# Gate and up projections of two token tiles by Strassen's scheme: seven products of quarters in place of eight

## The reference

```python
def fp4_quant_dequant(x):
    xb = x.reshape(shape[:-1] + (shape[-1] // BLOCK, BLOCK))     # BLOCK = 16
    scale = jnp.maximum(jnp.max(jnp.abs(xb), axis=-1, keepdims=True) / 6.0, 1e-12)
    q = _GRID[jnp.searchsorted(_MID, jnp.abs(xb / scale))] * jnp.sign(xb / scale) * scale
gate = fp4_linear(x, w_gate)          # 8192 tokens x 512, weights 1408 x 512
y = fp4_linear(x, w_up)
h = jax.nn.silu(gate) * y
return fp4_linear(h, w_down)          # 1408 -> 512
```

## Time and profile before

| | before |
|---|---|
| runs | 2209.19, 2212.1, 2213.11 us; median 2212.1 us |
| the profiled execution | 2211.99 us, its span 2209.8 us, mean granted clock 0.998 |
| busy: PE, DVE, POOL, ACT | 97%, 75%, 55%, 30% of the span |
| chain that ended last | PE 89%, DVE 4%, issue 3% |
| DMA | 251.82 MB, mean 114 GB/s |

### The profile page before, as it was taken

One profiled execution on the slowest core, in us unless ns is written; L12 is line 12 of the kernel. 1 busy time (PEld: TensorE's weight loads), 2 busy tenths in 40 slices (PEclk: granted clock), 3 DMA queues, 4 the chain that ended last, 5 costly groups with the idle time before them and its releaser, 6 DMA issues.

```text
span 2209.8 us, 46872 instructions
## 1 busy us (share of the span) xinstructions
PE 2152.9 (97%) x16712; PEld 1045.1 (47%) x16712; DVE 1663.1 (75%) x3108; ACT 657.1 (30%) x1009; POOL 1219.6 (55%) x877
## 2 busy tenths in 40 slices
PE   4999999999999989999999999999999999999999
PEld 1445454544545444444444444444444444444444
DVE  7777878778687665778778777787787877878774
ACT  3233333333343322222222222222222232222221
POOL 3266767676675544555555555555555555555553
PEclk9999999999999999999999999999999999999999
DMA  9656666585756444333333433333334333343333
GB/s 270 175 124 177 156 148 180 125 198 127 181 151 167 131 137 129 78 90 80 87 83 79 94 75 85 89 81 87 83 77 91 78 87 84 77 92 76 87 74 68
DMA packets 449418, 251.82 MB, mean 114 GB/s; under 512 B 367282, under 2 KB 373938, under 8 KB 449300
## 3 DMA queue, kind: packets, MB, share of 16 engines
q1 hardware_dynamic: 448404, 246.99, 46.0%
q10 hardware_dynamic: 576, 2.10, 0.2%
q0 software_dynamic: 320, 0.97, 0.2%
HBM read 99.01 MB, written 59.77 MB: 72 GB/s over the span
## 4 chain that ended last, share of the span: by engine, by line
PE 89%; DVE 4%; issue 3%; DMA 1%; SPq 1%; POOL 1%; ACT 0%; DVEq 0%; POOLq 0%; ACTq 0%
PE acc L977 19%; PE prj L1345 7%; PE ops L1345 7%; PE prj L977 6%; PE acc L1326 5%; PE acc L1330 5%; PE acc L1327 5%; PE prj L1347 3%; PE ops L1347 3%; PE acc L1328 2%; PE sps L1328 2%; PE sps L1331 2%; PE acc L1331 2%; PE sps L1329 2%; PE acc L1329 2%
## 5 line engine op out<-in xcount | busy, mean ns | idle before, releaser
L977 PE MATMUL acc<-late 128*128 128x512 f16 x2304 | 518.8, 382 | 15.0 <-DMA late<-xh 10.4
L977 PEld LDWEIGHTS acc<-late 128*128 128x128 f16 x2304 | 220.9, 98 | 281.8 <-issue 21.2
L208 POOL TENSOR_TENSOR qk<-qk,xh 128x1408 f32<-128x1408 f32 x64 | 165.7, 2590 | 230.0 <-DVE qk L245 230.0
L1220 DVE SCALAR_TENSOR_TENSOR qk<-acc,row_gains,xh 128x512 f32<-128x512 f32 x64 | 48.0, 751 | 260.4 <-ACT xh L1285 260.4
L203 POOL TENSOR_TENSOR qk<-qk,xh 128x1024 f32<-128x1024 f32 (+1 forms) x128 | 177.5, 1387 | 111.1 <-DVE xh L224 111.1
L213 POOL TENSOR_TENSOR v<-qk,v 128x1408 f16<-128x1408 f32 x64 | 183.1, 2860 | 100.3 <-ACT v L255 100.3
L1345 PE MATMUL prj<-late,qk 128*128 128x512 f16 x704 | 214.6, 379 | 0.7 <-DMA qk<-v 0.7
L1345 PE MATMUL ops<-late,qk 128*128 128x512 f16 x704 | 214.6, 379 | 0.0
L255 ACT ACTIVATE v<-qk 128x1408 f16<-128x1408 f32 x64 | 88.1, 1377 | 367.4 <-POOL qk L208 367.4
L1326 PE MATMUL acc<-late,turned 128*128 128x512 f16 x512 | 194.0, 379 | 0.4 <-DVE qk L1220 0.4
L1330 PE MATMUL acc<-late,turned 128*128 128x512 f16 x512 | 194.0, 379 | 0.0
(11 more groups left out here) (158 smaller groups left out, 4440.8 us busy)
## 6 DMA issues: line engine op xcount, KB each, us to landing
normed<-late SPq DMA_DIRECT2D x64, 256.0 KB, 2.7
res<-in_L_attn_x SPq DMA_DIRECT2D x64, 256.0 KB, 3.1
attended<-res SPq DMA_DIRECT2D x64, 256.0 KB, 2.6
raw<-normed SPq DMA_DIRECT2D x64, 256.0 KB, 2.7
v<-attended SPq DMA_DIRECT2D x64, 256.0 KB, 2.7
out<-v SPq DMA_DIRECT2D x64, 256.0 KB, 2.0
late<-in_L_attn_x SPq DMA_DIRECT2D x62, 256.0 KB, 3.9
ready<-turned SPq DMA_DIRECT2D x36, 256.0 KB, 2.3
```

Source lines behind the costliest of these rows:

```text
L208: pool.tensor_tensor(blocks(v), blocks(v), spread(s[3]), ALU.mult).then_inc(q["valued"], 1)
L977: last = pe.matmul(out, lhsT, rhs, start=(at == 0), stop=(at == n - 1))
```

## The change

Two tiles A1, A2 (rows) and their 512 channels are seen as a matrix of four quarters: a tile is a row of quarters, its channels 0 to 255 and 256 to 511 the columns. Gate and up of the weights are likewise four quarters, by channel half and by gate or up. The seven products of the Winograd form of Strassen's scheme give all four results (gate and up of both tiles), with four sums of rows, four sums of weights and seven sums of products a chunk.

- Weights: `sum_units` on POOL forms four sums of 128 x 256 for each group of gate and up units; four splits (4, 4, 6 and 4 blocks of 128) replace three, so `ready` and the places of the weights (`weight_places`) hold 14 blocks for gate and up where there were 8. The step strings of attention are new on all engines.
- Rows: both tiles of a pair are loaded, scaled with a joint row gain (`joint_gain`), and split in seven quarters (`low_rows`, `LEFT = 7`), after `sum_rows` on DVE.
- Products: `products` makes seven products of six matmuls a chunk. ACT copies the first three to SBUF (`copy_product`, tile `mc`). POOL adds `second_sum`, `fourth_sum` and `second_up`; DVE adds `third_sum`, `first_gate`, `first_up` and `second_gate`, each from a PSUM bank and an SBUF tile. `hidden` reads up and Silu from SBUF for both tiles. `freed` is what a bank's next product waits for.
- The hidden tile is quantised whole, 1408 columns at a time, in place of 1024 and 384.
- `periods` becomes `pairs`, which runs a step string for a pair of tiles: letter, number (tile of the pair, chunk or product), prime for the pair before, plus for the next one. On POOL `a`, `b`, `e` are the three sums, `s`, `v`, `l` rows, `S`, `V`, `L` hidden tiles. On DVE `m`, `j`, `q`, `w` are the rows' maxima, gain, rounding and sums; `u`, `g`, `c`, `d` the four sums from PSUM; `x`, `y` the hidden products; `B`, `Q`, `K` the hidden maxima, gain and rounding; `f` closes a tile.

The first gate and up products no longer stand in attention's list of TensorE, but in feed-forward's. The core of the diff:

```diff
-def periods(engine, step):
-
-    for t in range(4):
-        step(t - t % 2, t % 2)
-    with engine.Fori(2, NT // 2 - 2) as pair:
-        for k in range(2):
-            step(pair * 2, k)
-    for t in range(NT - 4, NT + DRAIN):
-        step(t - t % 2, t % 2)
+def pairs(engine, steps, do, begun):
+
+
+    def follow_pair(pair, q):
+        for step in steps.split():
+            shift = step.count("+") - step.count("'")
+            if isinstance(pair, int) and (not 0 <= pair + q + shift < NT // 2 or
+                                          pair + q + shift == 0 and step[0] in begun):
+                continue
+            do[step[0]](pair + (q + shift), (q + shift) % 2, int(step[1:].strip("+'")))
+
+    for pair in (0, 2):
+        for q in range(2):
+            follow_pair(pair, q)
...
-    dve.tensor_reduce(g[:, 0:1], s[1], AX.X, ALU.max).then_inc(q["row"], 1)
...
+        def sum_units(b, n):
+            g, half = n // 2, C // 2
+            (b11, b21), (b12, b22) = ((raw[:, m, 0:half], raw[:, m, half:]) for m in range(2))
+            if n % 2 == 0:
+                pool.wait_ge(f["valued"], at(b, PER, 3 * g + 1))
+                pool.wait_ge(f["low"], at(b, SPLITS, 4 * g))
+                pool.tensor_tensor(b11, b12, b11, ALU.subtract).then_inc(f_sum, 1)
+                pool.wait_ge(f_sum, at(b, SPLITS, 4 * g))
+                pool.tensor_tensor(b12, b22, b12, ALU.subtract).then_inc(f_sum, 1)
+            else:
+                pool.wait_ge(f["low"], at(b, SPLITS, 4 * g + 1))
+                pool.tensor_tensor(b12, b22, b11, ALU.subtract).then_inc(f_sum, 1)
+                pool.wait_ge(f_sum, at(b, SPLITS, 4 * g + 2))
+                pool.tensor_tensor(b21, b21, b12, ALU.subtract).then_inc(f_sum, 1)
+
+        def low_split(b, n):
+            pool.wait_ge(f["high"], at(b, SPLITS, n))
+            to = split_of(wh, n)
+            pool.tensor_tensor(to[:, 1], sources(n), to[:, 0], ALU.subtract).then_inc(f["low"], 1)
...
+        def turn_rows(p, q, n):
+            since(sp, xq["low"], p * 3 + (2 + n))
+            hold(sp, held)
+            since(sp, made, p * 21 - 21)
+            if second(p) and n == 0:
+                await_all(sp, ended.projected + ended.everything)
+            hold(sp, held)
+            lo, hi = (0, 3) if n == 0 else (3, LEFT)
+            sp.dma_start_transpose(xt[q][:, lo:hi].rearrange("p m a c t -> p (m a c) t"),
+                                   xh[:, lo:hi].rearrange("p m a c -> p (m a c)")).then_inc(xt_in[q], 16)
+
...
+        def low_rows(p, q, n):
+            if n == 0:
+                since(pool, xq["high"], p * 3 + 2)
+                pool.tensor_tensor(xh[:, 0:2, 1, :], halves(xr[:, 0, :]), xh[:, 0:2, 0, :],
+                                   ALU.subtract).then_inc(xq["low"], 1)
+                pool.tensor_tensor(xh[:, 2, 1, :], xr[:, 1, C // 2:], xh[:, 2, 0, :],
+                                   ALU.subtract).then_inc(xq["low"], 1)
+            else:
+                since(pool, xq["high"], p * 3 + 3)
+                pool.tensor_tensor(xh[:, 3:LEFT, 1, :], halves(xr.rearrange("p k c -> p (k c)")), xh[:, 3:LEFT, 0, :],
+                                   ALU.subtract).then_inc(xq["low"], 1)
+
+        def second_sum(p, q, c):
+            since(pool, copied, p * 9 + (3 * c + 2))
+            n = CHUNKS[c][1]
+            pool.tensor_tensor(mc[:, c % 2, 1, 0:n], mc[:, c % 2, 1, 0:n], mc[:, c % 2, 0, 0:n],
+                               ALU.add).then_inc(u2_done, 1)
+
+        def fourth_sum(p, q, c):
+            since(pool, copied, p * 9 + (3 * c + 3))
+            since(pool, u2_done, chunk(p, c))
+            since(pool, hq["low"], tile(p, 0) - 4)
+            if second(p) and c == 0:
+                await_all(pool, ended.projected)
+            s, n = cols(c)
+            pool.tensor_tensor(hv[q][:, 0, s], mc[:, c % 2, 1, 0:n], mc[:, c % 2, 2, 0:n], ALU.add).then_inc(u4_done, 1)
+
+        def second_up(p, q, c):
+            since(pool, u3_done, chunk(p, c))
+            since(pool, copied, p * 9 + (3 * c + 3))
+            since(pool, u4_done, chunk(p, c))
+            s, n = cols(c)
+            pool.tensor_tensor(mc[:, c % 2, 2, 0:n], hv[q][:, 1, s], mc[:, c % 2, 2, 0:n], ALU.add).then_inc(up1_done, 1)
+
+        def scale_hidden(p, q, k):
+            scale(pool, hq, hv[q][:, k, :], [hs[:, k, n, :] for n in range(4)], tile(p, k) - 1)
+
+        def value_hidden(p, q, k):
+            since(pool, hq["gained"], tile(p, k))
+            value(pool, hq, hv[q][:, k, :], [hs[:, k, n, :] for n in range(4)], tile(p, k) - 1)
+
+        def low_hidden(p, q, k):
+            low(pool, hq, hv[q][:, k, :], hh, tile(p, k) - 1)
...
+        def joint_gain(p, q, n):
+            g = xg[:, q, :]
+            since(dve, xq["scales"], p * 2 + 2)
+            dve.tensor_reduce(g[:, 0:1], xs[:, :, 1, :], AX.XY, ALU.max).then_inc(xq["row"], 1)
+            row_gain(dve, xq, g, p)
+            dve.tensor_scalar(xs[:, :, 3, :], xs[:, :, 1, :], g[:, 2:3], -SUM_TOP,
+                              ALU.mult, ALU.mult).then_inc(xq["gained"], 1)
+            dve.tensor_tensor(g[:, 3:4], g[:, 1:2], wsc[:, 4:5], ALU.mult).then_inc(xq["gains"], 1)
+
+        def round_rows(p, q, k):
+            rounded(dve, xq, xr[:, k, :], xm, tile(p, k) - 1)
...
+        def sum_rows(p, q, n):
+            h = C // 2
+            a11, a12, a21, a22 = xr[:, 0, 0:h], xr[:, 0, h:], xr[:, 1, 0:h], xr[:, 1, h:]
+            since(dve, xq["low"], p * 3 + 2)
+            dve.tensor_tensor(a22, a21, a22, ALU.add).then_inc(summed, 1)
+            dve.tensor_tensor(a21, a11, a21, ALU.subtract).then_inc(summed, 1)
+            since(dve, summed, p * 4 + 2)
+            dve.tensor_tensor(a11, a22, a11, ALU.subtract).then_inc(summed, 1)
+            since(dve, summed, p * 4 + 3)
+            dve.tensor_tensor(a12, a12, a11, ALU.subtract).then_inc(summed, 1)
+
+        def third_sum(p, q, c):
+            if c == 0 and (first(p) or second(p)):
+                await_all(dve, ended.attended if first(p) else ended.projected)
+            s, n = cols(c)
+            since(dve, made, product(p, c, 3))
+            since(dve, u2_done, chunk(p, c))
+            since(dve, hq["low"], tile(p, 1) - 4)
+            dve.tensor_tensor(hv[q][:, 1, s], bank(q, c, 3)[:, 0:n], mc[:, c % 2, 1, 0:n], ALU.add).then_inc(u3_done, 1)
+
+        def first_gate(p, q, c):
+            n = CHUNKS[c][1]
+            since(dve, made, product(p, c, 4))
+            since(dve, copied, p * 9 + (3 * c + 1))
+            since(dve, h_done[0], chunk(p, before(c)))
+            dve.tensor_tensor(sg[:, c % 2, 0, 0:n], bank(q, c, 4)[:, 0:n], mc[:, c % 2, 0, 0:n], ALU.add).then_inc(gate0_done, 1)
+
+        def first_up(p, q, c):
+            s, n = cols(c)
+            since(dve, made, product(p, c, 5))
+            since(dve, u4_done, chunk(p, c))
+            dve.tensor_tensor(hv[q][:, 0, s], bank(q, c, 5)[:, 0:n], hv[q][:, 0, s], ALU.add).then_inc(up0_done, 1)
+
+        def second_gate(p, q, c):
+            s, n = cols(c)
+            since(dve, made, product(p, c, 6))
+            since(dve, u3_done, chunk(p, c))
+            since(dve, h_done[1], chunk(p, before(c)))
+            dve.tensor_tensor(sg[:, c % 2, 1, 0:n], bank(q, c, 6)[:, 0:n], hv[q][:, 1, s], ALU.add).then_inc(gate1_done, 1)
+
+        def hidden(p, q, c, k):
+            s, n = cols(c)
+            since(dve, xq["gains"], p + 1)
+            if k == 0:
+                since(dve, up0_done, chunk(p, c))
+            else:
+                since(dve, up1_done, chunk(p, c))
+                since(dve, gate1_done, chunk(p, c))
+            since(dve, silu_done[k], chunk(p, c))
+            up = mc[:, c % 2, 2, 0:n] if k else hv[q][:, 0, s]
+            dve.scalar_tensor_tensor(hv[q][:, k, s], up, xg[:, q, 3:4], sg[:, c % 2, k, 0:n],
...
+                                     ALU.mult, ALU.mult).then_inc(h_done[k], 1)
...
+        def hidden_maxima(p, q, k):
+            since(dve, h_done[k], chunk(p, 2))
+            since(dve, hq["valued"], tile(p, k) - 2)
+            block_scales(dve, hq, hv[q][:, k, :], [hs[:, k, n, :] for n in range(4)], 1e-12,
+                         tile(p, k) - 1)
+
+        def hidden_gain(p, q, k):
+            g, s = hg[:, k, :], [hs[:, k, n, :] for n in range(4)]
+            since(dve, hq["scales"], tile(p, k))
+            dve.tensor_reduce(g[:, 0:1], s[1], AX.X, ALU.max).then_inc(hq["row"], 1)
+            row_gain(dve, hq, g, tile(p, k) - 1)
+            dve.tensor_scalar(s[3], s[1], g[:, 2:3], -SCALE_TOP, ALU.mult, ALU.mult).then_inc(hq["gained"], 1)
+            since(dve, final, tile(p, k) - 4)
+            dve.tensor_tensor(hk[:, 2 * q + k:2 * q + k + 1], g[:, 1:2], wsc[:, 5:6], ALU.mult).then_inc(hq["gains"], 1)
+
...
+        def freed(p, c, n):
+            if n < 2:
+                since(pe, copied, p * 9 + (3 * c + n - 1))
+            elif n < 6:
```

(48 more changed lines are left out.)

636 lines of the change are left out of this document (306 added, 330 removed), and 56 rows, old and new, of tables (dst, start, to, v).

## The result

The changed kernel takes 2568.95 us in the median of four runs (2567.89 to 2572.83); the kernel before takes 2211.75 us in four (2209.19 to 2213.11). The ratio is 1.162, 95% interval 1.160 to 1.164: slower by 357 us. The prediction was 2573 us.

A forecast was written before the change was run, and what follows sets the result against it. TensorE bound the kernel before; after the change, DVE and POOL excluding each other would. First product at 839, 32 pairs x 54 = 1728, end 4, plus 2.2 us outside the span: 2573 us, range 2360 to 2725.

The forecast's parts named there:

- DVE's 4 us a tile to give: Feed-forward before: DVE fills about 17 us of each tile, then waits some 4 us for the next product.
- DVE and POOL exclude each other: Feed-forward: POOL's instructions and DVE's two-SBUF-operand instructions or small tensor_scalars wait for each other; 52.5 us a pair before overlaps.
- The rival without effective exclusion: Feed-forward: POOL's sums slip between DVE's two-operand instructions, TensorE stays the bound at 39.2 us a pair; 2106 us, 5%.
- the one of proportional waits: Feed-forward: DVE's waits grow only in proportion to POOL's work, 43.4 us a pair, 2234 us; 3%.
- the floor: Feed-forward: orders fall so that nearly all is covered, 45 to 47.5 us a pair, 2285 to 2365 us; 12%.
- 54 us a pair: Feed-forward: period chosen for a pair of tiles, between the cover estimate's 50.5 us and the walk's 57.
- the walk: Feed-forward: both engines' lists followed in order; DVE waits 22.5 us on top of 34.6, 57 us a pair.
- the cover estimate: Feed-forward: 75% of DVE's other work and pauses covers POOL; 15.9 us waiting on top of 34.6, 50.5 a pair.
- The list of collisions: Feed-forward: where DVE waits for POOL, by instruction, such as row sums 4.7 us; 24.4 us a pair, less the heads.
- Attention, +3 us, bounds nothing and 55: Attention: POOL's new weight work delays the first product by 3 us; at most 55, all 9 us in six batches.
- The end, 4 us: After the last pair: both its tiles go through rounding before the last down projection, 4 us on top of full periods.
- The signs named ahead: Feed-forward profile after: TensorE about 72% busy, DVE near 100%, two-operand DVE and POOL records stretched, PSUM sums near 0.75 us.

The follow-up runs named there:

- the kernel with reductions in both kinds of places: Changed kernel, with feed-forward's long DVE instructions on two SBUF operands and eleven small tensor_scalars a pair as one-operand reductions: 2185.88 us, 39.2 us a pair.
- the four feed-forward experiments: Changed kernel with one-operand reductions for DVE's long two-operand instructions (2266.69 us), small tensor_scalars (2503.56), both (2185.88); or POOL's product sums cut to 8 columns (2423.62).
- the kernel before with 128 increments: Kernel before, with 128 semaphore increments that nothing waits for put ahead of TensorE's list, shifting its code: 2249.04 us, attention 843.2 us.
- the experiments: Changed kernel with POOL's attention weight sums cut to 8 columns (2558.89 us), DVE's edge copies as one-operand reductions (2555.94), or both (2557.2).

## Why the prediction was right, and where three terms were off

- **What TensorE gains, 39.2 us a pair.** Right; the kernel with reductions in both kinds of places shows it with TensorE full.
- **DVE's 4 us a tile to give.** A wrong reading of the earlier trace rows, without effect on the sum. In that wait DVE isn't held by TensorE's next product. The Silu that it waits for (L1285, at 1602.31) stands on ACT behind L255 (1601.03), which waited 5.74 us for POOL's L208 (1598.32), which waited 3.59 us for DVE's own rounding. In the kernel before this ring comes round in 21.10 us for the first 48 tiles or so, while TensorE takes 21.38, so in that order there was 0.3 us a tile to give, not 4. In the new order no ring binds above 39.2 us, as the kernel with both edits shows.
- **DVE and POOL exclude each other.** Right, by the two timelines and by the four feed-forward experiments. The rival without effective exclusion (2106 us) needed POOL and locked DVE work below 39.2 us; the one of proportional waits (43.4 us) and the floor (45 to 47.5) lie below 51.7. The Trainium skill's rule (SBUF — State Buffer, "Who interferes with whom"), by which a VectorE instruction with two SBUF inputs and a GpSimd instruction that reads SBUF lock each other out for the whole instruction, agrees for the long instructions (L282 at 1613.75 ends 1.48 us behind L242).
- **54 us a pair.** Measured 51.7; over 32 pairs the term was 74 us too large, and this was one of those that were off. Waits: each group's mean less its plain length (1585 and 652 for the roundings, 0.42 us for the sums, 0.68 for the products, 0.2 for small ones), times its number in a pair, gives hidden rounding 3.4, hidden gain 3.1, row scales 4.5, row sums 3.5, products 1.7, row rounding 0.8, hidden scales 0.8, one-element products 1.1, row gain 0.4: 19.3 us. That is the 19.4 that 54 less 34.6 stood for; the walk's 22.5 was 3 too many, the cover estimate's 15.9 3 too few. Own work: all record lengths of DVE add up to 550.2 us in 10.27 pairs, 53.5 a pair; less 19.3 it is 34.2, against 34.6. What was missed is that records overlap: a PSUM sum of 0.68 us is followed 0.61 later. The union of the same records is 521.6 us, so 2.8 us a pair of overlap, and DVE idles 0.9. 53.5 - 2.8 + 0.9 = 51.6, the 51.7 but for rounding. The prediction worked with start-to-start distance for the PSUM sums alone and added lengths elsewhere.
- **The list of collisions** was right in kind, less so in place. The row sums wait 3.5 us instead of 4.7, 2.5 of it in one of them (L1373). The one-element tensor_tensor that closes a gain was not on the list and waits too.
- **Attention, +3 us, bounds nothing and 55.** Measured 63.5, outside the bounds; this term failed. The bound counted POOL's new work alone, and by the table most of what came was of another sort. Of 62.7 us more, 34.8 are "issue", pauses whose place and size go with the position of the code; 14.6 are the same matmuls taking longer, at a mean granted clock of 0.97 instead of 0.99; 13.7 are waits for other engines, the kind that the term was about; shorter gaps are 0.4 less. In the kernel before with 128 increments the same three are 31.2, 10.6 and -3.4. So only the waits are shown to be the change's work, some 12 of the 13.7 us by the experiments; how much of the rest the new list would cost at a lucky position stays open.
- **The end, 4 us.** Measured 12.0. TensorE waits 13.5 us for the last pair's hidden tiles, and then begins at the lower clock: the granted clock is 0.50 from 2546.8 to 2550.4, which is 1.2 GHz, and 1.00 from 2551, which is 2.4. Its records are 0.43 us apart in the first stretch and 0.22 in the second:

```profile
2546.83 0.58 PE L1553 MATMUL ops<-late,wide 128*128 128x512 f16 x1 [13.51 <-DMA wide<-wide]
2547.21 0.63 PE L1556 MATMUL ops<-late,wide 128*128 128x512 f16 x1
2547.64 0.63 PE L1553 MATMUL ops<-late,wide 128*128 128x512 f16 x1
...
2551.08 0.38 PE L1556 MATMUL ops<-qk,wide 128*128 128x512 f16 x1
2551.30 0.38 PE L1553 MATMUL ops<-qk,wide 128*128 128x512 f16 x1
```

- **The sum.** Predicted 839 + 1728 + 4; measured 899.8 + 1654.7 + 12.0 = 2566.5, and 2.1 outside the span. -73, +61 and +8 nearly cancel: that the time came within 4 us is luck; that it lies well over 2500 us and not near 2200 is the exclusion.
- **The signs named ahead.** DVE near 100% (98), row sums well over 0.42 (up to 2.96), products over 0.69 (1.11), roundings over 1.6 (3.26), PSUM sums near 0.75 (0.68), POOL's 2.59 and 2.86 stretched: 3.32 and 3.63, but for L247, which stays at 2589 ns because it starts when DVE's rounding has just ended. TensorE's records fill 83% of the feed-forward window, not 72%, which was the share at 54 us and the full clock. 39.2 of 51.7 us is 76%, and at the mean granted clock of that window, 0.92, that makes 82%.

## What to carry to other kernels

Work on POOL and in DVE's two-operand instructions on SBUF goes into one common budget, and so do DVE's small tensor_scalars and f32 copies from SBUF to SBUF, though they have one operand. Add both engines' lists, take off what reads PSUM and the reductions and reciprocals, and compare that with the bound, before the matmuls saved are counted: here 34.8 and 17.7 us, against 39.2. Within the budget the number of alternations counts beside the length: a small instruction in the wrong place costs a whole one of the other engine, and when it is made harmless the next in line waits. And a difference of 1 to 2% between two kernels that share a long unrolled list of matmuls may be the position of the code alone (38 us of 2211 here); shift the list by some increments before it is explained.
